# A scan and an expert layer on one core: loop written out, first scan unit moved ahead, slot lists loaded per chunk

## What is computed

```python
def step(h, inp):
    u_t, d_t, b_t, c_t = inp
    dA = jnp.exp(d_t[..., None] * A)
    h = dA * h + (d_t * u_t)[..., None] * b_t[:, None, :]
    y = jnp.einsum('bdn,bn->bd', h, c_t)
    return (h, y)
...
h = jax.nn.silu(jnp.einsum('td,edh->eth', xt, w1)) * jnp.einsum('td,edh->eth', xt, w3)
y = jnp.einsum('eth,ehd->etd', h, w2)
```

## Time and profile before

| | |
|---|---|
| median of 3 runs | 818.84 us (816.11 to 818.92) |
| profiled execution, its own time | 817.38 us |
| span from its first to its last instruction | 815.3 us |
| mean granted TensorE clock | 0.913 |
| DVE busy | 682.9 us (84%), 882 instructions |
| PE busy | 663.9 us (81%), 4538 matmuls |
| POOL busy | 597.3 us (73%) |
| ACT busy | 431.0 us (53%) |
| DVE scans L1044 | 256 of 1267 ns |
| POOL products L534 | 308.0 us in all |
| gathers L486 | 71 of 1004 ns |
| most that all DMA queues moved in a slice of 20 us | 371 GB/s |
| tile adds L506, scan adds L516 | 71 of 1590 ns, 32 of 1577 ns |

### The profile page before, as it was taken

How to read it: one execution, slowest core, us unless ns; L and a number is a source line. 1 busy time by engine, 2 the same in 40 slices (tenths; PEclk the granted TensorE clock), 3 DMA queues, 4 the chain that set the end, 5 groups by cost and what they waited for, 6 DMA issues and landing times. The chain is left out here.

```text
span 815.3 us, 15751 instructions
## 1 busy us (share of the span) xinstructions
PE 663.9 (81%) x4538; PEld 422.7 (52%) x4539; DVE 682.9 (84%) x882; ACT 431.0 (53%) x926; POOL 597.3 (73%) x372
## 2 busy tenths in 40 slices
PE   3734889788998798989998898999889798989870
PEld 2523745245655465556655565565556555655550
DVE  5769777579999999999999999999999999997110
ACT  1324656465655556656655575566557554653320
POOL 3728800038788898988989898888989898889532
PEclk9866955599999989999999998999999998999995
DMA  7972659979944754674575466547645654662322
GB/s 228 371 259 91 180 206 297 321 221 241 210 102 103 144 118 87 146 150 94 115 163 111 89 149 138 105 90 164 139 90 125 134 127 90 142 142 35 49 27 26
DMA packets 76845, 118.63 MB, mean 146 GB/s; under 512 B 22456, under 2 KB 56848, under 8 KB 74512
## 3 DMA queue, kind: packets, MB, share of 16 engines
q1 hardware_dynamic: 54656, 90.95, 41.2%
q0 software_dynamic: 19824, 27.16, 19.4%
q10 hardware_dynamic: 2336, 0.15, 0.2%
HBM read 82.87 MB, written 35.27 MB: 145 GB/s over the span
## 5 line engine op out<-in xcount | busy, mean ns | idle before, releaser
L534 POOL TENSOR_TENSOR ring<-ring,bc 128x1024 f32<-128x1024 f32 (+2 forms) x128 | 308.0, 2424 | 38.9 <-DVE state L1047 38.0
L1044 DVE TENSOR_TENSOR_SCAN ring<-ring,state,pb 128x512 f32<-128x512 f32 x256 | 313.8, 1267 | 4.6
L654 ACT ACTIVATE ring<-late,aneg 128x512 f32<-128x512 f32 x256 | 164.2, 721 | 12.0 <-DMA late<-dd_d 9.1
L1035 DVE TENSOR_TENSOR pb<-fb,bc 128x1024 f32<-128x1024 f32 x128 | 157.3, 1229 | 3.0
L1284 PE MATMUL py<-w2x,pool 128*128 x568 | 141.6, 395 | 0.5 <-ACT pool L726 0.3
L1267 PE MATMUL fa<-w,pool 128*128 x284 | 137.7, 608 | 3.9 <-issue 2.8
L506 POOL DMA_INDIRECT out_dram<-pool,meta x71 | 112.9, 1590 | 29.8 <-issue 15.7
L1267 PE MATMUL fb<-w,pool 128*128 x284 | 134.3, 596 | 0.0
L486 POOL DMA_INDIRECT pool<-xn_d,meta x71 | 71.3, 1004 | 81.3 <-DVE ids L1001 33.5
L1284 PEld LDWEIGHTS py<-w2x,pool 128*128 128x128 f32 x568 | 107.7, 200 | 13.6 <-issue 1.0
L1267 PEld LDWEIGHTS fb<-w,pool 128*128 128x128 f32 x284 | 54.5, 192 | 68.9 <-issue 68.9
(11 more groups left out here) (213 smaller groups left out, 752.8 us busy)
## 6 DMA issues: line engine op xcount, KB each, us to landing
late<-dd_d SPq DMA_DIRECT2D x256, 128.0 KB
bc<-bc_d SPq DMA_DIRECT2D x72, 256.0 KB
w<-in_L_ffn_w_dram SPq DMA_DIRECT2D x16, 512.0 KB, 8.6
ring<-in_L_attn_x_dram SPq DMA_DIRECT2D x8, 512.0 KB, 4.3
out_dram<-ring SPq DMA_DIRECT2D x8, 512.0 KB, 7.7
xn_d<-w2x SPq DMA_DIRECT2D x8, 512.0 KB, 8.6
dd_d<-pool SPq DMA_DIRECT2D x8, 512.0 KB
dd_d<-ring SPq DMA_DIRECT2D x8, 512.0 KB, 5.1
```

The source lines that it names most:

```text
L534: ins = po.tensor_tensor(r, r, c_rows, ALU.mult)
L654: ins = ac.activation(ring[:, g % RING, n, :], dd[:, g % 2, 0, :], ACT.Exp, scale=aneg[:, NH * g + n:NH * g + n + 1])
L1035: ve.tensor_tensor(pb[:, :].rearrange("p (n c) -> p n c", n=2), pd[:, :].rearrange("p (o c) -> p o c", o=1).to_broadcast([P, 2, CH]), b_ro ...
L1044: ve.tensor_tensor_scan(r, r, pb[:, CH * m:CH * m + CH], state[:, NH * g + n:NH * g + n + 1], ALU.mult, ALU.add).then_inc(S["scan_done"], 1)
```

## The change

- The Fori loops of all engines are replaced by straight code over u = 0 to 63. All addresses are constants. The second slot of `ya` replaces `yb` and `hand_over`.
- On DVE and ACT unit 0 comes first: silu(u - 1) stands ahead of unit u. Tiles 63 to 70 remain behind the last unit. exps(0) no longer waits for the last stores. exps(1) waits for `bc_put1` and `dd_put10`, exps(2) for `dd_put11`.
- Slot lists are loaded 8 tiles at a time, once per chunk, in SP's g = 7.
- SP's waits for turned rows are gone. In chunk 0 the weight loads of an expert now follow load_dd, with no wait of their own for u = 0 and 1.
- Buffers: 6 for gathered rows (was 4), 3 for tile results (was 2). Gathers are issued 6 tiles ahead of the add (was 4).
- Behind the last unit the four scan adds are issued together, all waiting for tile 65. DVE multiplies states 2 and 3 of the last unit by C, POOL states 0 and 1. For tiles from 66 on the rows are turned into `pb`, the products' bank, and turn_h stands between the two products of `up`.

```diff
+            def load_meta(b):
+                at = BLOCK * (b % 2)
+                sp.dma_start(meta[:, at:at + BLOCK, :].rearrange("p j c -> p (j c)"),
+                             tab[:, BLOCK * b:BLOCK * b + BLOCK, :].rearrange("p j c -> p (j c)")).then_inc(S["meta_in"], 16)
...
-            turn(0)
-            with sp.Fori(1, NCH) as c:
-                turn(c)
...
+            for u in range(UNITS):
+                c, g = u // G, u % G
+                if u >= 2:
+                    load_dd(u)
+                if c == 0 and g + EARLY < E:
+                    load_up(g + EARLY, w3, w3_in)
+                    load_down(g + EARLY)
...
+                if g >= 4 and c + 1 < NCH:
+                    load_bc(c + 1, g - 4)
+                if g == 7 and c:
+                    sp.wait_ge(S["meta_in"], 16 * (c + 1))
+                    sp.wait_ge(S["added"], landed_expert(BLOCK * c - 1))
+                    load_meta(c + 1)
...
+            def gather(j):
+                po.wait_ge(S["meta_in"], 16 * (j // BLOCK + 1))
+                if j >= XR:
+                    po.wait_ge(S["xtr_done"], j - XR + 1)
...
+            for u in range(UNITS):
+                c, g = u // G, u % G
+                j = u - 2
+                if j >= 0:
+                    gather(j + XR)
...
+                po.wait_ge(S["h_ready"], u + 1)
+                done = multiply(u, slice(0, split))
+                for n in scans:
+                    add_scan(c - 1, n, landed_scan(c - 1, scans[0]) - 16)
...
+                if j >= 0:
+                    add_expert(j)
+            for j in range(UNITS - 2, FT):
+                if j + XR < FT:
+                    gather(j + XR)
+                add_expert(j)
+                if j == LAST_SCANS:
+                    for n in range(TPC):
+                        add_scan(NCH - 1, n, landed_expert(j))
...
+            put_du(0)
+            exps(0)
+            evac_xt(0)
+            exps(1)
+            for u in range(1, FT + 1):
+                j = u - 1
+                tanh(j)
+                if u < UNITS:
+                    put_du(u)
...
+            for u in range(UNITS):
+                if u:
+                    silu(u - 1)
+                half_unit(u, 0)
+                half_unit(u, 1)
+                keep_states(u)
```

More of the change, by code:

```diff
@@ L33 @@
 RING = 4
[L34 to L38, removed]
+UNITS = NCH * G
+REST = UNITS + 1
+SCAN_UNITS = {3: (0, 1), 7: (2, 3)}
+XR, XT, YE = 6, 4, 3
+BLOCK = G
 CONST_LOADS, CONST2_LOADS = 5, 8
@@ L243, in apart, with experts_by, scans_by, unit_of_expert @@
             eng.sem_inc(S["passed"], 1)
[L245 to L265, removed]
+        def experts_by(u):
+            return max(0, u - 1)
+        LAST_SCANS = UNITS + 1
+        def scans_by(u):
+            c, g = u // G, u % G
+            return 0 if c == 0 else (c - 1) * TPC + sum(len(SCAN_UNITS[k]) for k in SCAN_UNITS if k <= g)
+        def unit_of_expert(j):
+            return min(j + 2, UNITS - 1)
+        def landed_expert(j):
+            return 16 * (1 + j + 1 + scans_by(unit_of_expert(j)) + (TPC if j > LAST_SCANS else 0))
+        def landed_scan(c, n):
+            u = (c + 1) * G + next(k for k in SCAN_UNITS if n in SCAN_UNITS[k])
+            return 16 * (1 + experts_by(u - 1) + c * TPC + n + 1)
         @block.sync
@@ L541, in _ @@
-            turn(0)
-            with po.Fori(1, NCH) as c:
-                turn(c)
-            for i, (kind, n) in enumerate(REST_ADDS):
-                if kind == "expert":
-                    if n + 4 < FT:
-                        gather(n + 4, (n + 4) % SPI)
-                    add_expert(REST_TURN + i, n, n % SPI, n % 2)
-                else:
-                    add_scan(REST_TURN + i, NCH - 1, n)
-            po.wait_ge(S["added"], landed(REST_TURN + len(REST_ADDS) - 1))
+            for j in range(2, XR):
+                gather(j)
@@ L752, in turn @@
-            def turn(c):
-                exps(c, 0)
-                for s in range(SPI):
-                    j = SPI * c + 1 + s
-                    tanh(j, (s + 1) % 2)
-                    put_du(c, s)
-                    evac_ht(j - 1)
-                    take_units(c, s)
-                    ac.wait_ge(S["b_done"], j)
-                    evac_xt(j + 1, (s + 2) % 4)
-                    if s + 1 < SPI:
-                        exps(c, s + 1)
-                    if s == 2 and not isinstance(c, int):
-                        hand_over(c - 1)
-                    evac_y(j - 1, s % 2, s, expert_turn(c, s - 2) if s >= 2 else
-                           None if isinstance(c, int) else expert_turn(c - 1, SPI - 1) - (1 - s))
```

502 lines of the change are left out of this document (199 added, 303 removed).

## The result

The changed kernel is slower. Its median is 825.75 us (822.44 to 826.97, 4 runs) beside 818.28 for the kernel before on the same chip, a ratio of 1.009 with a 95% interval of 1.0052 to 1.0127. The profiled execution took 822.44 us (span 820.7). The rival "slower, by the slot list" came, at three quarters of its price (17.1 us for 23 in the middle).

A forecast was written before the change was run, and what follows sets the result against it. DVE was taken to bound the middle, with the start and the end's chain of adds exposed. -7.3 - 6.2 + 4.0 + 1.5 = -8.0 us, so 818.84 - 8.0 = 810.8 us, range 801 to 820.

The forecast's parts named there:

- slower, by the slot list: Rival: list lands late in 7 chunks, PE waits, its clock falls, 23 us reach DVE; +11, 830 us; chance 0.12.
- the start: Ahead of unit 2: unit 0 runs beside the stores' landing, -8.9; load_dd(2) late behind weights, +1.6; sum -7.3 us.
- the loops: DVE's units in the middle: straight code keeps chunk 0's pitch of 8.89 us, so the loop cost goes, -6.2 us.
- the buffers: More buffers, no hand_over: takes waits off ACT beside DVE's scans, worth 0 on the path.
- the end: Chain of adds behind unit 63's state copy: last add at +61.2 instead of 59.7 us, +1.5 (bounds 0 and +6).
- the slot list's first half: Around unit 44: list issued at 576.5, landing at 580.2 behind 1 MB, so POOL's product starts late and PE waits 1.9 us.
- The estimate from that page's rates: Slot list behind the megabyte: 2.0 us fixed plus bytes at 436 GB/s, landing at 578.1 and no cost.
- so the wait is hidden: Slot list, chunks without a clock fall: PE's 1.9 us wait stays within the tanh's 3.0 us slack before DVE.
- +4.0: Slot list: falls of the clock now reach DVE, twice the 2.1 us they cost before (bounds 0 and 12).
- POOL stays 1 to 3 us later than before all the time: Slot list in the middle: POOL barely catches up per chunk, PE's slack shrinks by as much; priced within the 4 us.

The follow-up runs named there:

- both mends: The best version: changed kernel with the slot list issued ahead of load_dd's DMAs in g = 7 and expert e's weights loaded in unit g = e; 804.19 us, 0.9808.
- before, DVE straight: Kernel before with only DVE's two loops written out as straight code, other engines keeping theirs; 814.77 us, ratio 0.9945.
- list ahead: Changed kernel with the slot list still loaded in g = 7, but issued between load_dd's waits and its DMAs; 806.48 us, ratio 0.9867.
- list one unit earlier: Changed kernel with the slot list of 8 tiles loaded in SP's g = 6 instead of g = 7; 807.03 us, ratio 0.9868.
- unit 0 waiting: The both mends version with unit 0's exps again waiting for the last stores of delta and of B and C; 809.07 us, ratio 0.9861.
- no list: Changed kernel without slot list loads; POOL and ACT take slot addresses and gate weights from `tab` directly; 807.88 us, ratio 0.9875.
- last scan adds in a row: The both mends version with the four last scan adds each waiting for the landing of the one before; 812.73 us, ratio 0.9907.
- list in the middle: Changed kernel with the slot list issued between the unit's delta load and the quarter of B and C; 812.8 us, ratio 0.9896.
- weights late: Changed kernel with chunk 0's W3 and W2 loads of expert e issued in unit g = e, not g = e - 2; 822.81 us, ratio 1.0064.
- few products on PE: Changed kernel with extra 128x512 products on PE in chunks 1 to 7, 3 at g = 3 and 2 at g = 4; 829.09 us, ratio 1.0112.
- POOL late: The both mends version with 6 extra 128x256 products on POOL ahead of the gather at g = 4 of chunks 1 to 7; 828.17 us, ratio 1.0108.
- many products on PE: Changed kernel with 5 extra 128x512 products on PE ahead of the fold at g = 3, 4 and 7 of chunks 1 to 7; 853.4 us, 1.0403.

## Why the prediction was wrong

**Right: the start.** -7.3 was forecast, -7.1 came. The mechanism held: the waits of unit 0 and the wait for load_dd(2) are each shown by their own experiment. The closeness of the sum is part luck. Unit 1's copy stood at 177.3 (178.4 forecast), so the gain was 9.9 us for 8.9, and the wait for load_dd(2) took 2.9 us for 1.6. Unit 0's copy came at 168.26, not near 165: its delta, which I had as there earlier, let ACT start only at 158.84.

**Right: the loops, the buffers and the end.** The steps at each chunk are gone, and between waits the pitch is 8.89. No new wait on a buffer shows. The adds took 60.7 us from the last state copy for 61.2 forecast. These terms sum to what was forecast within 0.3 us (the end with what follows it: 1.6 for 1.5), so the whole error lies in the middle.

**Right in its mechanism: the slot list's first half.** The list was issued as forecast, some 1 us behind the state copy (1.6 in unit 20), and landed in a median of 4.0 us, between my two ends of 1.7 and 4.8. The gather then came 5.1 to 6.6 us behind the state copy in six chunks of seven, where I had +4.6 (580.2 - 575.6). The Trainium skill (DMA: Bandwidth & Descriptors, Queues, rings and completion order) has each engine consume a ring's descriptors in order. The traces agree with that: 1.7 us ahead of the megabyte, 2.2 to 2.6 behind its first half, a median of 4.0 behind all of it. The estimate from that page's rates put the landing 2.5 us behind the state copy and the cost at nothing. The list landed some 5 to 6 us behind it. The page gives these rates for DMAs that GpSimd issues, and the loads here are SP's.

**The step that failed: "so the wait is hidden", and "+4.0".** I read PE's slack as the 3.0 us between a tanh and DVE's wish for it, added that PE can catch up, and priced the lost cover at twice what falls had cost before. It was 17.1 us, above the upper bound of 12 too. Two things were wrong in it.

First, PE's room. The share of 81% told me that it had much. But that is the mean over the whole span. Between the state copies of units 2 and 63 PE was busy for 489.7 of 550.8 us, 89%. And even that says too much. The timeline of PE in the kernel before shows two starts of `up` with no wait for POOL between them:

```profile
579.92 1.88 PE L1267 MATMUL fa<-w,pool 128*128 x4
...
588.02 1.88 PE L1267 MATMUL fa<-w,pool 128*128 x4
```

This step of PE takes 8.10 us and a unit of DVE 8.89. It is a floor: some 20 of the steps of the middle take 8.04 to 8.11 us, in this kernel and in the changed one, and none is shorter. The room is 0.79 us per step, 48 us in 61 units, and a microsecond of wait needs more than one step to be made good.

Second, the clock isn't a separate matter. A fall of 6.8 us at half the clock costs PE up to 3.4 us, over four steps of room, and a wait in the same chunk then finds no slack. In the four versions with the list in time or without one (one unit earlier, ahead, none, both mends) a fall of 6.8 us cost DVE 0.4 to 1.6 us and a short one (3.4 us) at most 0.3. In the changed kernel it was 1.0 to 4.4 us and up to 3.0. This table is bookkeeping from the traces between units 2 and 63, in us: PE's waits for POOL (190 to 745 us), half the time at the lower clock, extra products on PE, and DVE's loss.

| kernel | waits | half of low clock | extra | sum | loss |
|---|---|---|---|---|---|
| before, DVE straight | 14.9 | 12.0 | 0 | 26.9 | 2.4 and 3.0 of loops |
| list ahead | 20.4 | 8.5 | 0 | 28.9 | 1.7 |
| both mends | 21.3 | 8.5 | 0 | 29.8 | 2.3 |
| before | 17.0 | 13.7 | 0 | 30.7 | 2.1 and 6.2 of loops |
| list one unit earlier | 19.9 | 12.0 | 0 | 31.9 | 3.2 |
| unit 0 waiting | 20.9 | 12.0 | 0 | 32.9 | 2.9 |
| no list | 21.8 | 13.7 | 0 | 35.5 | 3.7 |
| last scan adds in a row | 24.9 | 13.7 | 0 | 38.6 | 5.9 |
| list in the middle | 22.1 | 18.8 | 0 | 40.9 | 9.7 |
| after | 27.6 | 20.5 | 0 | 48.1 | 19.2 |
| weights late | 34.4 | 18.8 | 0 | 53.2 | 20.7 |
| few products on PE | 15.5 | 17.1 | 32.3 | 64.9 | 25.8 |
| POOL late | 35.1 | 30.7 | 0 | 65.8 | 26.3 |
| many products on PE | 1.9 | 0 | 89.1 | 91.0 | 43.6 |

The loss goes roughly by the sum, whatever it is made of. In part this is plain arithmetic, since PE's time in the stage is its own work, these terms and its waits for ACT. The versions with few products on PE and with POOL late have nearly the same sum and the same loss, one with six falls and extra work, the other with eleven and none. Up to a sum of 31 DVE loses about 2 us, and from 39 on the loss climbs fast, before the whole room of 48 is used up, since a step that ends early can't be banked for a later wait. What the sum is above the loss is what PE's own slack took up: in the versions in straight code 27 to 33 us in most, 39 in two, and 47 in the last, where PE is busy nearly throughout. That is the room of 48, found a second way. The kernel before stood near the edge, and a list that let POOL gather 3 to 5 us late in six of the seven chunks pushed it over.

**The rival that came true.** "Slower, by the slot list" named the mechanism (PE waits behind its wait at g = 3, the clock falls, the slack is gone, 3.3 us per chunk). Seven waits for a late list did come, with eight falls, and 2.2 to 4.4 us of loss behind five of them. But the falls came where POOL's split products are, and only two right behind a late list's own wait: by the places of the waits and falls, what carried most of the loss was POOL's lateness in the units behind. The prediction had that ("POOL stays 1 to 3 us later than before all the time") and priced it at 4 us. The rival's chance was 0.12 for want of the row on PE's step. Its condition was 1.7 us per chunk. PE's waits for POOL rose by 10.6 us and the time lost at the lower clock by 6.8, together 2.5 us per chunk, against a room of 0.79 us per step (6.3 per chunk) of which waits and falls had taken 4.4 before.

**What stays open.** That the late list causes the loss is shown: moved ahead, moved a unit earlier or taken out, it is gone, and POOL made late without it brings it back. How much of the 17 us comes through the falls and how much through PE's waits is only in the bookkeeping: between "list ahead" and the changed kernel the waits rose by 7.2 us and half the time at the lower clock by 12.0. No run changes one and keeps the other. The number of falls also varies between traces of kernels that don't differ in the middle (three and six in two of them), and there is one trace of each.

## What to carry to other kernels

Take an engine's room from the shortest period of its step against the pitch of the bounding engine, and not from its busy share, least of all from one over the whole span. Put a small load that someone needs soon ahead of the large ones on its queue. And count TensorE's waits and the falls of its clock as one debt against the same slack: in this kernel a late helper engine was paid for in both. When you add work on purpose to test a cause, read its real length from the trace before you read the result.

## What the hardware showed unexpectedly

- A load of 8 KB took 1.7 us in 7 of 7 cases with nothing of its step ahead of it on its queue, 2.2 to 2.6 behind 512 KB, and a median of 4.0 (2.3 to 4.8) behind 1 MB.
- A fall of the clock reaches DVE late: where one cost DVE over 1 us, the state copy of the unit that it slowed most came 11 to 14 us behind its end. Many falls cost DVE nothing that shows.
- With PE kept busy for 560.6 of 587 us the granted clock was 1.00 throughout, and the kernel was the slowest of all.
- One fp32 product of 128x512 is two records of 0.446 us each in the profile, 0.89 us in all. Counting records as products halves the price.
- Indirect adds that wait for each other start 4.57 us apart, those issued together 1.87, and the next one starts 4.4 us (4.6 in the best version) behind the last of four, so in these traces adds in flight side by side didn't land slower.
